# Scores of the 32-wide heads: two stationary tiles that hold the high and the low part of a head pair side by side

## What is computed

```
xn = rmsnorm(x, norm_w)
q = (xn @ wq).reshape(B, T, N_HEADS, HEAD_DIM)            # 16 heads of 32
k = (cond @ wk).reshape(B, S, N_KV_HEADS, HEAD_DIM)       # 4 kv heads
qg = q.reshape(B, T, N_KV_HEADS, n_rep, HEAD_DIM)
scores = jnp.einsum('btgrd,bsgd->bgrts', qg, k) * scale
attn = jax.nn.softmax(scores.astype(jnp.float32), axis=-1)
out = jnp.einsum('bgrts,bsgd->btgrd', attn, v).reshape(B, T, N_HEADS * HEAD_DIM)
return residual + out @ wo
```

## Time and profile before

| | us |
|---|---|
| median of 3 runs | 2091.65 (2091.45 to 2092.06) |
| the profiled execution | 2090.98 |
| its span in the trace | 2089.2 |
| PE busy | 2044.5 (98%) |
| DVE busy | 1390.2 (67%) |
| ACT busy | 966.1 (46%) |
| POOL busy | 644.7 (31%) |

### The profile page before, as it was taken

The page is one execution under the profiler, slowest core; times in us unless marked ns, Lnnn a source line. Parts: engine busy times, 40 slices in busy tenths (PEclk is TensorE's granted clock), DMA queues, the critical chain, the costliest instruction groups (busy, mean ns, idle before and its releaser), DMA issues.

```text
span 2089.2 us, 31293 instructions
## 1 busy us (share of the span) xinstructions
PE 2044.5 (98%) x11546; PEld 1765.7 (85%) x11546; DVE 1390.2 (67%) x2408; ACT 966.1 (46%) x1814; POOL 644.7 (31%) x519
## 2 busy tenths in 40 slices
PE   8999999999999998999999999999999989999998
PEld 8999988888888886788888888888888867888886
DVE  5332365775568555888888676557755675888885
ACT  3222253553445344655554554335534553555552
POOL 1000042322232254454443341223222443444441
PEclk9999999999999999999999999999999999999999
DMA  7788832222122222343333332212221222333322
GB/s 214 168 171 200 190 91 63 72 67 73 53 72 70 65 75 68 92 108 93 93 90 94 104 96 64 77 53 71 66 73 52 73 85 67 80 91 86 85 72 82
DMA packets 262393, 191.02 MB, mean 91 GB/s; under 512 B 197506, under 2 KB 199970, under 8 KB 259682
## 3 DMA queue, kind: packets, MB, share of 16 engines
q1 hardware_dynamic: 262242, 189.03, 34.6%
HBM read 132.66 MB, written 56.26 MB: 90 GB/s over the span
## 4 chain that ended last, share of the span: by engine, by line
PE 90%; DVE 6%; ACT 1%; DMA 1%; issue 1%; SPq 1%; POOL 0%; DVEq 0%; ACTq 0%
PE acc_bank L846 11%; PE acc_bank L241 8%; PE acc_bank L243 8%; PE acc_bank L242 8%; PE q_bank L804 8%; PE q_bank L808 8%; PE q_bank L806 8%; PE t_bank L826 7%; PE ctx_bank L241 4%; PE ctx_bank L242 4%; PE ctx_bank L243 4%; PE s_bank L767 2%; PE s_bank L241 2%; PE s_bank L764 2%; PE s_bank L770 2%; PE s_bank L243 2%
## 5 line engine op out<-in xcount | busy, mean ns | idle before, releaser
L1262 POOL TENSOR_TENSOR prob<-prob,rinv 128x1232 f32<-128x1232 f32 x128 | 288.5, 2254 | 1044.1 <-DVE rinv L1152 1044.1
L1014 ACT ACTIVATE q_s<-q_bank 128x512 fp32r<-128x512 f32 x192 | 115.1, 599 | 532.9 <-PE q_bank L808 527.0
L846 PE MATMUL acc_bank<-pT_s,vals_s 128*128 128x512 f32 x1024 | 338.1, 415 | 0.0
L1110 DVE TENSOR_REDUCE mx<-s_bank 128x4 f32<-128x308 f32 x512 | 240.5, 470 | 125.7 <-PE s_bank L243 63.5
L804 PE MATMUL q_bank<-x_s,w_s 128*128 128x512 f32 x768 | 319.2, 416 | 4.0 <-POOL w_s L1255 4.0
L808 PE MATMUL q_bank<-x_s,w_s 128*128 128x512 f32 x768 | 313.9, 409 | 0.0
L806 PE MATMUL q_bank<-x_s,w_s 128*128 128x512 f32 x768 | 312.9, 407 | 0.0
L241 PE MATMUL acc_bank<-o_s,w_s 128*128 128x512 f32 x752 | 303.6, 404 | 2.5 <-DVE o_s L1143 2.5
L243 PE MATMUL acc_bank<-o_s,w_s 128*128 128x512 f32 x752 | 296.8, 395 | 0.0
L242 PE MATMUL acc_bank<-o_s,w_s 128*128 128x512 f32 x752 | 296.7, 395 | 0.0
L1005 ACT ACTIVATE prob<-prob,rstd 128x308 f32<-128x308 f32 x256 | 141.2, 555 | 287.3 <-DVE prob L1114 271.5
(11 more groups left out here) (107 smaller groups left out, 4097.2 us busy)
## 6 DMA issues: line engine op xcount, KB each, us to landing
stream<-x_back SPq DMA_DIRECT2D x128, 256.0 KB, 2.6
x_front<-stream SPq DMA_DIRECT2D x96, 256.0 KB, 3.4
x_back<-stream SPq DMA_DIRECT2D x96, 256.0 KB, 4.0
kvw_raw<-kvw SPq DMA_DIRECT2D x17, 1024.0 KB, 8.4
k_scr<-k_out SPq DMA_DIRECT2D x36, 308.0 KB, 9.2
keys_s<-k_scr SPq DMA_DIRECT2D x128, 77.0 KB, 2.4
v_scr<-v_out SPq DMA_DIRECT2D x8, 1024.0 KB
vals_s<-v_scr SPq DMA_DIRECT2D x512, 6.5 KB
```

The source lines that it names most:

```text
L846: mm = pe.matmul(out, w, pT_s[:, part], start=i == mine[0] and part == 2 * n and w is v[0], stop=i == mine[-1] and w is terms[-1][0] and p ...
L1110: dve.tensor_reduce(top, scored, AX_X, ALU.max).then_inc(s_max, 1)
L1262: pool.tensor_tensor(view, view, rinv[:, slot].unsqueeze(2).broadcast_to([P, TILES * GH, CTX]), ALU.mult).then_inc(p_norm, 1)
```

## The change

In B units the two q tiles that the scores use are laid out anew. `q_s[:, slot, 0, 0]` stays the high part of all four heads. The two halves of `q_s[:, slot, 1]` become one tile for each pair of heads: on the pair's own 64 partitions its high part, on the other 64 its low part. Since the four heads of a B unit share their keys, the high part of the keys needs 154 columns (two heads), and the same 154 columns serve both pairs. A tile of scores is then two products of 154 columns (high and low part of a pair against the keys' high part) and one of 308 (high part against the keys' low part): 616 moving columns.

To fill these tiles ScalarE makes two copies of 64 partitions beside the copy of 128, and VectorE makes its subtraction as two of 64 partitions; each of the two reads one half of the partitions and writes the other. The four key loads of a unit write other columns and are otherwise as before.

```diff
--- before.py
+++ after.py
@@ -670,9 +670,9 @@
                                      k_scr[4 * p + g, b, 64 * e:64 * e + 64].rearrange("q c h n -> q (c h) n"))\
                           .then_inc(keys_loaded[slot], 16)
                 else:
-                    keys = keys_s[:, slot].bitcast(F32).rearrange("q (h n) -> q h n", h=2)
                     for r in range(GH):
-                        sp.dma_start(keys[32 * r:32 * r + 32, :, CTX * r:CTX * r + CTX],
+                        keys = keys_s[32 * r:32 * r + 32, slot, 0:2 * CTX * (2 + r - r % 2)].bitcast(F32)
+                        sp.dma_start(keys.rearrange("q (h a n) -> q h a n", h=2, n=CTX)[:, :, r % 2],
                                      k1_scr[p, b, 32 * g:32 * g + 32]).then_inc(keys_loaded[slot], 16)
 
             def load_vals(u):
@@ -777,9 +777,11 @@
                     if t == 0:
                         pe.wait_ge(q_out, plan.q[("q", u, 0)] + 1)
                         pe.wait_ge(keys_loaded[slot], plan.keys_count(u))
-                    keys = keys_s[:, slot].rearrange("q (h n) -> q h n", h=2)
-                    three_passes(pe, out[:, 0:SC], [q_s[:, slot, h, 0, tok] for h in range(2)],
-                                 [keys[:, h] for h in range(2)], True, True).then_inc(s_mm, 1)
+                    for pair in range(2):
+                        pe.matmul(out[:, PAIR * pair:PAIR * (pair + 1)], q_s[:, slot, 1, pair, tok],
+                                  keys_s[:, slot, 0:PAIR], start=pair == 0, stop=False, skip_group_check=True)
+                    pe.matmul(out[:, 0:SC], q_s[:, slot, 0, 0, tok], keys_s[:, slot, PAIR:PAIR + SC], start=False,
+                              stop=True, skip_group_check=True).then_inc(s_mm, 1)
                     yield
 
             def queries(u):
@@ -1011,7 +1013,12 @@
                     act.wait_ge(q_mm, item + 1)
                     if m == 0 and u >= 2:
                         act.wait_ge(s_mm, TILES * (u - 2) + TILES)
-                    act.activation(q_s[:, u % 2, 0, m], q_bank[item % 2][:, :], ACT.Copy).then_inc(q_hi, 1)
+                    high = act.activation(q_s[:, u % 2, 0, m], q_bank[item % 2][:, :], ACT.Copy)
+                    if kind(u).name == "B":
+                        for pair in range(2):
+                            rows = slice(64 * pair, 64 * pair + 64)
+                            high = act.activation(q_s[rows, u % 2, 1, pair], q_bank[item % 2][rows, :], ACT.Copy)
+                    high.then_inc(q_hi, 1)
                     yield
 
             def split_t(u, n):
@@ -1118,8 +1125,15 @@
                 for m in range(kind(u).Q):
                     item = plan.q[("q", u, m)]
                     dve.wait_ge(q_hi, plan.q_splits[("q", u, m)] + 1)
-                    dve.tensor_tensor(q_s[:, u % 2, 1, m], q_bank[item % 2][:, :], q_s[:, u % 2, 0, m].bitcast(F32),
-                                      ALU.subtract).then_inc(q_out, 1)
+                    if kind(u).name == "A":
+                        low = dve.tensor_tensor(q_s[:, u % 2, 1, m], q_bank[item % 2][:, :],
+                                                q_s[:, u % 2, 0, m].bitcast(F32), ALU.subtract)
+                    else:
+                        for pair in range(2):
+                            rows, other = slice(64 * pair, 64 * pair + 64), slice(64 - 64 * pair, 128 - 64 * pair)
+                            low = dve.tensor_tensor(q_s[other, u % 2, 1, pair], q_bank[item % 2][rows, :],
+                                                    q_s[rows, u % 2, 0, m].bitcast(F32), ALU.subtract)
+                    low.then_inc(q_out, 1)
                     yield
 
             def rest_t(u, n):
```

## The result

The kernel after takes 2123.02 us (median of 4 runs, 2120.0 to 2126.06), the kernel before beside it 2091.86 us. The ratio is 1.0151 (95% interval 1.0137 to 1.0165): 31 us slower. The forecast was 2112.5 us with a range up to 2119. So the direction was right, the size was short by 10.5 us, and the time lies 4 us above the range. The profiled execution after took 2121.19 us, 30.2 more than the one of before.

What follows compares the result with a forecast made beforehand. TensorE was taken as the bound, coupled to VectorE once a unit. 2090.98 + 11.3 (steady units) + 9.6 (border steps) = 2111.9 us, 2112.6 on the median, stated as 2112.5; own range 2107 to 2118, full range 2093 to 2119.

Steps and rivals of the forecast that it cites:

- the tile and what it brings: TensorE's score tile in B units: 0.42 to 0.36 us, saving 0.06; of 0.24 saved a unit, 0.12 is left.
- The formula for an isolated product: Skill page's 154/2.4 + 2.5 = 67 ns per narrow score product; by itself a 38 us saving, which the prediction rejected.
- VectorE's price: Two held half-height subtractions and the held `rest_o`: 1.71 in place of 0.71, so +1.00 us a unit.
- the rival of 14%: VectorE's half-height subtractions overlap like other instructions: +0.60 us a unit, total 2094.3 us; chance 14%.
- the coupling: Once a unit TensorE's fourth score tile waits for VectorE's second difference, 0.10 us before the change.
- The recursion over four units: VectorE's lateness passed between steady units, plus 0.33 at the projection: 43.74 us against 42.90, +0.84 for four.
- The elastic rival: Lateness averages out, so four steady units cost VectorE's own chain, 42.75 us; total 2099 us; chance 10%.
- the one in which the slack takes it all: VectorE's idle 7 us in four units absorbs the 4 us added; TensorE keeps its saving: 2076 us; chance 6%.
- the term 2 x 4.8 = 9.6 for the borders: Steps 32 to 36 of both B layers: VectorE's added 1.00 each, less 0.2 in step 34, +9.6 us.
- They cost nothing: ScalarE's half-height copies end by T + 7.6, before VectorE wants them at T + 8.0, T being the unit's first score product.
- the rival "above 2119": ScalarE's copies come late in the border steps, or VectorE's price is 1.1 a unit: above 2119 us; chance 4%.
- In steps 32 to 36 the full 1.00 passes to the end: Where VectorE already bounds both B layers, its added 1.00 us a unit fully lengthens the run, less 0.2 in step 34.

Runs made afterwards that it cites:

- the two pairs of runs: Copies removed against copies kept: with VectorE's two subtractions 2117.16 against 2123.02 us; with one full-height subtraction 2085.80 against 2090.65 us.
- narrow tiles alone: Changed kernel without ScalarE's two extra copies and with VectorE's subtraction as one of 128 partitions: 2085.80 us, ratio 0.9976.
- the run meant to do so: Changed kernel plus nine unread products of 512 columns in each of steps 32 to 36 and 96 to 100, where TensorE waits: 2127.26 us, ratio 1.018.
- two lines moved: Kernel before, with only one of the three value products moved ahead of the third score tile: 2083.71 us, ratio 0.9972.
- the pair in the borders alone: Changed kernel with copies and two subtractions only in the first six units of each B layer, one subtraction elsewhere: 2105.95 us, ratio 1.0077.
- copies signalled apart: Changed kernel with the two extra copies read from the first copy in SBUF, under a semaphore only TensorE waits for: 2121.11 us, ratio 1.0146.
- steady units only: Changed kernel with copies and two subtractions only from each B layer's seventh unit on, one subtraction before: 2102.21 us, ratio 1.0052.

## Why the forecast was right in direction and short in size

**Right: the tile and what it brings.** 0.37 against 0.36 a tile. The sum held though its terms fell otherwise: the two narrow products take 1885.40 - 1885.21 = 0.19 together and the wide one 0.18, where the forecast had 0.22 and 0.14. 0.43 of 0.96 us in four units reached the end, against 0.48 forecast, because the fourth tile is bound to VectorE. The formula for an isolated product that the prediction quotes from the Trainium skill would have made the saving 38 us; here two narrow products in a row take 0.19 us and not twice 67 ns.

**Right: VectorE's price.** 1.00 a unit from the earlier trace rows, measured 1.00, and with the halves uncrossed 0.60, which was the price that the rival of 14% had put on the pair as it is. The rows of another operation on the same engine were a good witness, since they had the same property, the output in another half than the input.

**Right: the coupling.** The recursion over four units (lateness 0.48, 0, 0.48, 0 and the 0.33 at the projection) gave 43.74; 43.84 came, unit by unit within 0.07. Undone alone, this part is 11.7 us against 11.3. The elastic rival (42.75) and the one in which the slack takes it all (no wait at the fourth tile) fall with it.

**Wrong: the term 2 x 4.8 = 9.6 for the borders.** It measured 20 us, and this is what put the time outside the range. Two statements failed.
- "They cost nothing", of ScalarE's copies. I had read the cover at T + 5.90 in a steady unit and used it for all 64. In the borders the queries are made right ahead of their use, in most steps with no projection in between, so the copies lie on the path: 4.9 and 5.9 us by the two pairs of runs (the second is 5.1 if each is read against the kernel before beside it). The forecast had this, at 4%, as the rival "above 2119", and it is the one that came. The path there could have been read: in the kernel before, VectorE in time order waits for ScalarE's `q_s` at the start of step 31, 1.07 us:

```profile
785.64 0.69 DVE L1121 TENSOR_TENSOR q_s<-q_bank,q_s 128x512 fp32r<-128x512 f32 x1 [1.07 <-ACT q_s L1014]
```

- "In steps 32 to 36 the full 1.00 passes to the end". It took only VectorE's added time, at an unchanged speed of TensorE. Without the copies a border is already 111.9 and 112.4, against 104.1 and 107.1 for the narrow tiles alone: 6.6 on the mean and not 4.8. In the second border, where the granted clock is 0.94 in both runs, the pair costs 112.4 - 107.1 = 5.3 us. In the first it costs 7.8, the clock is 0.95 against 0.98, and the same 478 products are busy 95.24 us instead of 92.14. That speaks for the clock as the cause of the excess, a cost that the forecast put at nothing. Its share was not separated, and the run meant to do so did not settle it.

Adding up from the profiled executions: 11.6 in the steady units; in the two borders 0.9 for the narrow tiles (which saved nothing there), 13.1 for VectorE's pair where 9.6 was forecast, and 5.7 for the copies where nothing was; 31 us in all.

## What to carry to other kernels

Cost an edit separately in each stretch of a program where the order of work differs, and above all where a stage begins: "hidden" read in a steady unit says nothing of the first units of a layer. On VectorE count an instruction that changes partitions as one full duration, and its successor too; the same two half-height operations cost 0.60 more uncrossed and 1.00 more crossed. And before making the bound engine's work smaller, look at the order at the point where it is tied to another engine: two lines moved gave 0.3% without any new instruction.

## What the runs showed of the hardware that was not expected

- ScalarE has a dearer start as well. In the border the whole-height copy is followed by the next after 784.42 - 783.92 = 0.50, and the two half-height ones, in different halves, take 1.18 together. No run has them in the same half, so what makes them dearer is not shown.
- A kernel's time moves with the granted clock from one execution to the next: 9.5 us over the four executions with the pair in the borders alone, at 0.993 down to 0.986. Within one execution the two borders have the same number of products; 0.98 and 0.94 go with 104.06 and 107.13 us (narrow tiles alone), 0.96 and 0.90 with 113.77 and 117.74 (copies signalled apart), some 0.7 us for each 0.01. But 0.97 and 0.97 go with 105.94 and 104.46 (steady units only), so the mean clock alone does not set a border's time.
- GpSimd's crossing copy of 64 x 512, from SBUF, is 0.64 us (1.28 for two), no slower than VectorE's held subtraction from PSUM (0.71).
